# A cross-attention and expert kernel on one core: the beginning in another order, with weights loaded into the places of their low parts

## The reference

```python
q = (layernorm(x) @ Wq + bq)          # 16 heads of 32
k = (y @ Wk + bk); v = (y @ Wv + bv)  # 77 keys for each batch
attn = softmax(q k^T / sqrt(32))
x = x + relu((attn v) @ W1 + b1) @ W2 + b2          # W1 512x1024, W2 1024x512
...
xt = layernorm(x); top1 = argmax(xt @ Wg.T)
xhat = (xt - mu) * rsqrt(var + 1e-5)
y = gelu((xhat * s_e + b_e) @ w1 + bb1) @ w2 + bb2  # for the expert e = top1
x = x + y
```

## Time and profile before

| | |
|---|---|
| time, median of 3 runs | 1514.02 us (1513.26 to 1514.06) |
| the profiled execution | 1511.64 us, its span 1509.8 us, mean granted TensorE clock 0.988 |
| PE, DVE, ACT, POOL busy | 97%, 68%, 47%, 29% of the span |
| HBM read and written | 76.24 MB and 46.72 MB, 81 GB/s over the span |
| first `H` matmul of the first block | 89.38 us after the span's start |

### The profile page before, as it was taken

One profiled execution on the slowest core, in us unless ns is written; L12 is line 12 of the kernel. 1 busy time (PEld: TensorE's weight loads), 2 busy tenths in 40 slices (PEclk: granted clock), 3 DMA queues, 4 the chain that ended last, 5 costly groups with the idle time before them and its releaser, 6 DMA issues.

```text
span 1509.8 us, 23959 instructions
## 1 busy us (share of the span) xinstructions
PE 1467.3 (97%) x7764; PEld 1225.1 (81%) x7764; DVE 1034.0 (68%) x2521; ACT 713.5 (47%) x2015; POOL 431.2 (29%) x312
## 2 busy tenths in 40 slices
PE   7689999999999999999999999999999999999997
PEld 4578888888888787878788888888888878778896
DVE  5845757685867677676767686758575766558666
ACT  3534535363635364545445353635353635434554
POOL 2512131222222222212121212222222222127776
PEclk9799999999999999999999999999999999999999
DMA  9310020213020202122120301120202011558873
GB/s 237 116 56 29 1 84 1 85 28 109 15 91 29 91 29 86 42 68 60 32 88 22 99 22 57 41 89 1 84 1 84 1 57 56 188 182 285 252 232 119
DMA packets 77327, 122.70 MB, mean 81 GB/s; under 512 B 28367, under 2 KB 36832, under 8 KB 76183
## 3 DMA queue, kind: packets, MB, share of 16 engines
q1 hardware_dynamic: 66406, 87.47, 20.1%
q0 software_dynamic: 10800, 33.70, 5.8%
HBM read 76.24 MB, written 46.72 MB: 81 GB/s over the span
## 4 chain that ended last, share of the span: by engine, by line
PE 91%; DVE 4%; ACT 2%; issue 1%; DMA 1%; POOL 1%; POOLq 0%; DVEq 0%; SPq 0%; ACTq 0%
PE bank L1138 24%; PE bank L1160 23%; PE bank L956 11%; PE bank L1090 8%; PE bank L980 7%; PE bank L1053 4%; PE bank L1562 4%; PE bank L1606 4%; PE bank L1229 2%; PE bank L1545 2%; PE bank L924 2%; PE bank L1207 1%; DVE actH L1071 1%; DMA w_raw<-in_W 1%; ACT actH L1065 1%
## 5 line engine op out<-in xcount | busy, mean ns | idle before, releaser
L1160 PE MATMUL bank<-w,actH 128*128 128x512 f32 x1536 | 371.2, 393 | 0.0
L1138 PE MATMUL bank<-actA,w 128*128 128x512 f32 x1536 | 371.0, 395 | 0.0
L1138 PEld LDWEIGHTS bank<-actA,w 128*128 128x128 f32 x1536 | 285.0, 188 | 61.6
L1160 PEld LDWEIGHTS bank<-w,actH 128*128 128x128 f32 x1536 | 283.2, 188 | 54.8
L1047 POOL TENSOR_TENSOR E<-E,rc 128x1232 f32<-128x1232 f32 x64 | 145.0, 2265 | 435.0 <-DVE rc L1041 435.0
L1304 POOL DMA_INDIRECT region<-rows,pos x64 | 63.7, 995 | 457.5 <-DVE pos L1298 419.0
L956 PE MATMUL bank<-actA,wq 128*128 128x512 f32 x768 | 182.0, 390 | 0.0
L1145 ACT ACTIVATE actH<-bank,b 128x512 fp32r<-128x512 f32 x128 | 88.3, 690 | 195.8 <-PE bank L1138 195.8
L1020 ACT ACTIVATE E<-bank,mx 128x77 f32<-128x77 f32 x512 | 157.6, 365 | 40.3 <-DVE mx L989 40.3
L956 PEld LDWEIGHTS bank<-actA,wq 128*128 128x128 f32 x768 | 144.2, 188 | 30.4 <-issue 0.5
L970 DVE SCALAR_TENSOR_TENSOR actQ<-bank,bq,actQ 128x512 fp32r<-128x512 f32 x64 | 48.0, 750 | 160.0 <-ACT actQ L965 160.0
(11 more groups left out here) (168 smaller groups left out, 2055.5 us busy)
## 6 DMA issues: line engine op xcount, KB each, us to landing
rowB<-region SPq DMA_DIRECT2D x71, 258.0 KB, 3.6
xn<-in_x SPq DMA_DIRECT2D x64, 256.0 KB, 2.9
rows<-in_x SPq DMA_DIRECT2D x64, 256.0 KB, 3.2
e_raw<-in_E SPq DMA_DIRECT2D x16, 256.0 KB, 3.1
region<-padrow SPq DMA_DIRECT2D x9, 258.0 KB, 2.7
w_raw<-in_W SPq DMA_DIRECT2D x1, 2048.0 KB, 10.4
w_raw<-in_W SPq DMA_DIRECT2D x2, 1024.0 KB, 8.2
e_parts<-e_high SPq DMA_DIRECT2D x8, 256.0 KB, 2.0
```

Of the source, the lines that this page charges most:

```text
L1138: mm = pe.matmul(p[:], w, a, start=k == 0 and j == 0, stop=k == KD - 1 and j == 2)
L1160: mm = pe.matmul(p[:], a, w, start=m == 0 and j == 0, stop=m == MF - 1 and j == 2)
```

## The change

Only the beginning is altered, up to the first layer of block 0.

- The four loads of `xn` are issued first, then the setup's loads; `W1` and `W2` are loaded in it too, without a wait. `XSTAT`'s chain is emitted in one go ahead of the keys, and `XT` stands between the second and the third `KP`.
- `wq_raw`, `w1_raw` and `w2_raw` are now the low places of `wq`, `w1` and `w2`, so that a low part is the loaded weight minus its high part, in place. The low part of `wq` is made by DVE and no longer by POOL; `W1` is split in four parts of 1024 columns (ACT and POOL), two of 2048 before; `W2` in four parts of 1024, during `H` 1 to 4 of block 0, high parts by ACT and low parts by DVE. `GATE` goes to `H` 5.
- Batch 0's keys go from `k_hl` to `kbd` by four ACT copies on 32 partitions each (`KCOPY`), and no longer through DRAM; its values go from `v_hl` to `vbd` by the 24 transfers directly.
- `VP` 0 stands ahead of `Q`; `VP` 1 to 3 stand in among the scores, with `Q` 2 and 3. `XB`, `ZERO_ROWS` and `XLOAD 1` go behind the attention of block 0.

```diff
+    o[0] = w2_at
     wv_raw = staged("wv_raw", [P, KT, D])
     ctxT = staged("ctxT", [P, KT, NB * M])
...
+    wq_raw = at("wq_raw", [P, KD, D], F32, wq_at + 4 * KD * D)
+    w1_raw = at("w1_raw", [P, KD, F], F32, w1_at + 4 * KD * F)
+    w2_raw = at("w2_raw", [P, MF, D], F32, w2_at + 4 * MF * D)
...
-        step("SETUP")
+
         step("XNLOAD", 0, 0)
         step("XNLOAD", 0, 2)
+        step("SETUP")
         step("XSTAT", 0)
+        step("DRIP", SUB)
+        step("BKS")
+        step("DRAIN")
         for m in range(KD):
             step("KP", m)
-        step("DRAIN")
+            if m == 1:
+                for s in range(SUB):
+                    step("XT", 0, s)
+        step("CONV_WQ")
         step("KSTORE")
-        step("CONV_WQ")
...
+        step("KCOPY")
+        step("VP", 0)
         step("VLOAD", 0, 0)
         step("VLOAD", 0, 1)
-        step("XLOAD", 0)
-        for m in range(KD):
-            step("Q", 0, m)
-            if m in (1, 2):
-                step("CONV_W1", m - 1)
-        step("GATE")
+        step("MASKS")
+        step("Q", 0, 0)
+        step("Q", 0, 1)
+        step("CONV_W1", 0)
         for g in range(KD):
             for s in range(SUB):
                 step("S", 0, g, s)
-            if g == 2:
-                step("CONV_W2", 0)
             step("EXP", 0, g)
             if g:
                 step("SUM", 0, g - 1)
-        step("CONV_W2", 1)
-        step("ZERO_ROWS")
-        step("XLOAD", 1)
-        for s in range(SUB):
-            step("XB", 0, s)
+                step("CONV_W1", g)
+            if g + 2 < KD:
+                step("Q", 0, g + 2)
+            if g + 1 < NB:
+                step("VP", g + 1)
+                step("VSTORE", g + 1)
+        step("XLOAD", 0)
...
+            if b == 0:
+                for s in range(SUB):
+                    step("XB", 0, s)
+                step("ZERO_ROWS")
+                step("XLOAD", 1)
...
+                if b == 0 and 1 <= m <= 4:
+                    step("CONV_W2", m - 1)
+                if b == 0 and m == 5:
+                    step("GATE")
...
+        def dve_bks(dve):
             dve.wait_ge(L["first"], 16 * NFIRST)
             dve.tensor_scalar(bks[:], bk[:], SCALE, None, ALU.mult).then_inc(S["dve_bks"], 1)
...
+        def act_kcopy(act):
+
+            act.wait_ge(S["pool_zero"], 1)
+            act.wait_ge(S["act_k"], KD)
+            act.wait_ge(S["dve_k"], KD)
+            for h in range(HG):
+                q = slice(HD * h, HD * h + HD)
+                act.activation(kbd[q, :, :, M * h:M * h + M], k_hl[q, :, :, 0:M], ACT.Identity).then_inc(S["act_kbd"], 1)
...
+        def dve_conv_wq(dve):
+            dve.wait_ge(S["act_wq"], 1)
+            dve.tensor_tensor(flat(wq[:, 1]), flat(wq_raw[:]), f32(flat(wq[:, 0])), ALU.subtract
+                              ).then_inc(S["dve_wq"], 1)
...
+        def pool_conv_w1(pool, k):
+            pool.wait_ge(S["act_w1"], k + 1)
+            pool.tensor_tensor(w1[:, 1, k, :], w1_raw[:, k, :], f32(w1[:, 0, k, :]), ALU.subtract
+                               ).then_inc(S["pool_w1"], 1)
...
+                pe.wait_ge(S["act_kbd"], HG)
+                if b >= BPB:
+                    pe.wait_ge(ld_k, 16 * KLOADS * (b // BPB))
...
             if b == 0 and j == 0:
-                act.wait_ge(S["pool_wq"], 1)
-                act.wait_ge(S["pool_w1"], 2)
-                act.wait_ge(S["w2_lo"], 1)
+                act.wait_ge(st_k, 16 * 2 * (NB - 1))
+                act.wait_ge(S["act_kbd"], HG)
```

More of the change, by code:

```diff
@@ L154, in staged @@
         return at(name, shape, dt, o[0] - size(shape, dt))
+    o[0] = E_at
     wk_raw = staged("wk_raw", [P, KT, D])
+    c_raw = staged("c_raw", [P, 2 * P])
+    assert o[0] <= E_at + size([P, KD, SUB, SC], F32)
+    o[0] = w2_at
     wv_raw = staged("wv_raw", [P, KT, D])
     ctxT = staged("ctxT", [P, KT, NB * M])
[L159 to L166, removed]
+    v_f = [staged(f"v_f{i}", [M, D]) for i in range(2)]
+    bvbc = staged("bvbc", [M, D])
+    assert o[0] <= w2_at + size([P, MF, D], F32)
+    o[0] = actH_at
     k_hl = staged("k_hl", [P, 2, KD, NB * M], F32R)
     k_f = staged("k_f", [P, KD, NB * M])
[L169 to L172, removed]
+    assert o[0] <= actH_at + size([P, 2, SLOTS, BLK], F32)
+    wq_raw = at("wq_raw", [P, KD, D], F32, wq_at + 4 * KD * D)
+    w1_raw = at("w1_raw", [P, KD, F], F32, w1_at + 4 * KD * F)
+    w2_raw = at("w2_raw", [P, MF, D], F32, w2_at + 4 * MF * D)
+    assert NB == 4
+    v_hl = [at(f"v_hl{i}", [M, 2, D], F32R, (rows_at[1], xn_at)[i // 2] + i % 2 * size([M, 2, D], F32))
+            for i in range(NB)]
+    assert 2 * size([M, 2, D], F32) <= min(size([P, SUB, ROW], F32), SUB * size([P, D], F32))
     e1 = at("e1", [P, KD, NE, EH], F32, wq_at)
@@ L649, in sp_kstore @@
             for h in range(2):
-                for i in range(NB):
+                for i in range(1, NB):
                     sp.dma_start(k_parts[i, h].rearrange("g p k -> p g k"),
@@ L666, in sp_vload @@
         def sp_vload(sp, i, part):
-            if part == 0 and i == 0:
-                for n_, s_ in enumerate(st_vs):
-                    sp.wait_ge(s_, 16 * (NB // 2))
+            if i == 0:
+                sp.wait_ge(S["act_v"], 1)
+                sp.wait_ge(S["dve_v"], 1)
                 sp.wait_ge(S["pool_zero"], 2)
-            if i:
+            else:
+                sp.wait_ge(st_v, 16 * (NB - 1))
                 sp.wait_ge(S["pe_av"], 3 * NP * BPB * i)
             for c, r, k, m, h in PIECES:
-                src = v_parts[i, part, k:k + m, :].rearrange("k (g h f) -> k g h f", g=NP, h=PH)[:, :, h, :]
+                src = v_parts[i, part, k:k + m, :] if i else f32(v_hl[0][k:k + m, part, :])
                 o_ = HD * (h % HG)
-                sp.dma_start(f32(vbd[r:r + m, part, :, c, o_:o_ + HD]), src).then_inc(ld_v, 16)
+                sp.dma_start(f32(vbd[r:r + m, part, :, c, o_:o_ + HD]),
+                             src.rearrange("k (g h f) -> k g h f", g=NP, h=PH)[:, :, h, :]).then_inc(ld_v, 16)
         KLOADS, VLOADS = HG * KD, 2 * len(PIECES)
@@ L682, in sp_vstore @@
             sp.wait_ge(S["dve_v"], i + 1)
[L683 removed]
+            sp.dma_start(v_parts[i].rearrange("s k f -> k s f"), f32(v_hl[i][:])).then_inc(st_v, 16)
         def sp_e1raw(sp, e):
@@ L830, in pool_conv_wq @@
-        def pool_conv_wq(pool):
-            pool.wait_ge(S["act_wq"], 1)
-            hi, lo = (wq[:, h].rearrange("p k n -> p (k n)") for h in range(2))
-            pool.tensor_tensor(lo, wq_raw[:], f32(hi), ALU.subtract).then_inc(S["pool_wq"], 1)
-        def w1_half(h, i):
-            n = KD * F // 2
-            return w1[:, h].rearrange("p k n -> p (k n)")[:, n * i:n * i + n], w1_raw[:, n * i:n * i + n]
-        def act_conv_w1(act, i):
-            act.wait_ge(L["w1"], 16)
-            hi, raw = w1_half(0, i)
-            act.activation(hi, raw, ACT.Identity).then_inc(S["act_w1"], 1)
@@ new lines, in xattn_moe_kernel, with w2_part, act_conv_w2 @@
+        NW2 = 4
+        def w2_part(t, i):
+            n = MF // NW2
+            return flat(t[:, n * i:n * i + n, :])
+        def act_conv_w2(act, i):
+            act.wait_ge(L["w2"], 16)
+            act.wait_ge(S["dve_v"], NB)
+            act.activation(w2_part(w2[:, 0], i), w2_part(w2_raw, i), ACT.Identity).then_inc(S["act_w2"], 1)
+        def dve_conv_w2(dve, i):
+            dve.wait_ge(S["act_w2"], i + 1)
+            dve.tensor_tensor(w2_part(w2[:, 1], i), w2_part(w2_raw, i), f32(w2_part(w2[:, 0], i)), ALU.subtract
+                              ).then_inc(S["dve_w2"], 1)
@@ L1014, in act_s @@
                 return
+            if b == 0 and s == 0:
+                act.wait_ge(S["dve_tri"], 1)
             if b and s == 0:
@@ L1636, in xattn_moe_kernel @@
             "SETUP": {"sp": sp_setup, "pool": pool_setup, "dve": dve_setup},
+            "BKS": {"dve": dve_bks},
+            "MASKS": {"dve": dve_masks},
+            "KCOPY": {"act": act_kcopy},
             "XLOAD": {"sp": sp_xload},
```

102 lines of the change are left out of this document (32 added, 70 removed).

## The result

The changed kernel takes 1517.47 us (1515.24 to 1520.93, 14 runs) where the kernel before takes 1513.49 (1511.07 to 1514.89, 14 runs): 1.003 of its time, 95% interval 1.0022 to 1.0039. I had forecast 1504.6. It is slower, by 0.3%.

What follows compares the result with a forecast made beforehand. PE was taken as busy 97%, leaving idle or half-clock time before block 0's first `H`: -5.9 at `Q` and -3.5 from `Q` to `H` make -9.4, profiled 1511.64 to 1502.2, median 1504.6, range 1500.5 to 1510.

Steps and rivals of the forecast that it cites:

- The change touches only what stands ahead of that `H`, and the streams behind it stay: Block 0's first `H`, at 89.38 before: only its start time, forecast 80.0, and fitting work among `H` 1 to 5 matter.
- What is put behind: Work moved behind the first `H`: `W2`'s parts fit under `H`, row statistics slip about 1.3 with room, added wait nothing.
- my five rivals: Slow clock at first Q, dearer score phase, late loads (0.26 together), more won (0.14), slower than before (0.04).
- The one on the other side, half clock in the score phase: Scores: PE never gets full clock, `H` at 96.7, 7.3 late, 1521 us; chance 0.04.
- Up to the first Q: Block 0's start, loads to first `Q`: `Q` starts at 25.8 against 31.73, 5.9 sooner.
- the 4.48 hold: Before the first `Q`: a small DVE instruction held 4.48 beside POOL's low part of `Wq`; forecast gone.
- my first rival: PE's clock down at the first Q, taking 5.7: `H` at 83, 1507.5 us; 0.26 shared with two other rivals.
- my own signs of being wrong: PE waiting for DVE in `H`, clock 0.50 in 26 to 45, or a load ending a wait behind 20 us.
- From Q to H: Scores through `AV` to first `H`: 3.5 sooner, 9.8 + 4.5 of waits gone, new work and a 1.7 hold put in.
- The hold: `VP` 3: DVE's subtraction of `v_hl` held beside POOL's `W1` part, some 2.3 instead of 0.69, making `H` 1.7 later.
- the bounds: Spread around `H` at 80.0, between 76 and 85; full clock in last transposes and `AV` would give 3.3.
- the added wait: Ahead of each later group of scores: 60 fulfilled waits behind queued matmuls cost nothing, or 1.2 if bared.

Runs made afterwards that it cites:

- The gap alone: The kernel before with only 128 unused bytes per partition added ahead of `kbd`: 1529.89 us against 1515.63, 1.0098 of it.
- the change without the gap: The changed kernel with `wg_raw` allocated behind all other tiles, order and waits untouched: 1504.40 us, 0.9925 of the kernel before.
- `AV` aligned: The changed kernel with tiles reordered, `wg_raw` last, and the distance of `vbd` and `actH` meant as a multiple of 256 bytes too: 1502.06 us, 0.9913 of before.

## Why the prediction was wrong, point by point

**The step that failed** is "The change touches only what stands ahead of that `H`, and the streams behind it stay", and with it "What is put behind" as the whole account of the blocks behind. Their instructions stay; what one of them costs did not. 240 of the 512-column products of a block went from 226.7, 229.0 and 228.3 ns to 232.5, 232.3 and 232.4: 48 x 5.8 + 96 x 3.3 + 96 x 4.1 = 990 ns, and the block grew by 0.95 to 1.0. The gap alone gives the loss, and the change without the gap gives the gain, so it is shown that the 128 bytes between the weights and the tiles behind them are the cause. Why a distance that is not a multiple of 256 bytes slows a product is not: no record tells what PE waits for inside a matmul. The Trainium skill, "SBUF — State Buffer", "SBUF: two separate sides", says that PE never waits on anyone, and "TensorE: Matmul & The Clock Gate", "Step-by-step: what each phase is for", that loading the next weights takes nothing from the running matmul's reads. Read so, a tile's place would not matter to PE. The 1529.89 of the gap alone shows that here it does, and the measurement decides; whether PE's own two reads collide, no run here shows.

**None of my five rivals had it.** The one on the other side, half clock in the score phase, did not occur: from 31 to 55 every window shows 1.00. The clock fell again only behind the scores, and was at 0.50 for the first 4.1 of `AV`'s 6.97; before shows that too (0.50 in the windows from 71 to 75, then 0.89 and 1.00).

**Up to the first Q** (-5.9 forecast, -4.7 measured). `bks` 11.34 for 11.2; the first normalised rows at 14.7 for 14.9; the 4.48 hold gone, as forecast. Mis-sized in this trace: `Wk` at 10.50 for 8.6, and two key projections of 6.37 in all for 5.1, so that `XT` began at 16.71 for 14.9, without the wait of 1.2; the low part of `Wq` ended at 26.90 for 25.8. Part of this is the execution: with `wg_raw` last, `Wk` lands at 10.09, the two projections take 5.12 and `Q` starts at 25.33.

**The clock at the first Q** was my first rival, and came in half its size. The windows of the changed kernel (PEclk is the granted clock as a share of 2.4 GHz):

```profile
core 0: us, PE busy (x) PEld busy (x) DVE busy (x) ACT busy (x) POOL busy (x), PEclk, DMA share, GB/s
...
25.00:27.00 2.00, 0.00 (x0) 0.03 (x1) 2.00 (x2) 1.93 (x4) 0.00 (x0) 0.96 1.01 251
27.00:29.00 2.00, 2.00 (x5) 1.61 (x6) 1.30 (x4) 1.05 (x2) 0.00 (x0) 0.50 1.38 124
29.00:31.00 2.00, 2.00 (x8) 1.58 (x7) 0.16 (x2) 0.00 (x0) 0.00 (x0) 0.68 1.36 117
...
71.00:73.00 2.00, 2.00 (x6) 1.52 (x6) 1.97 (x4) 1.01 (x2) 0.00 (x0) 0.50 0.00 0
```

After 2.70 idle the clock is 0.50 until some way into 29 to 31, and the 24 `Q` take 7.30; 24 `Q` take 5.74 at full clock in this kernel, so 1.5 are lost where I had 2.9. With `wg_raw` last they took 5.72 after the same 2.70. A clock of 0.50 in 26 to 45 was one of my own signs of being wrong, and it came, in 27 to 29 and part of 29 to 31.

**From Q to H** (-3.5 forecast, -3.0 measured, with those 1.5 in it). The hold has its 2.46 for 2.3, and 0.69 once POOL's part stood behind it. So the rule that I weighed there (the Trainium skill, "SBUF — State Buffer", "Who interferes with whom") agrees with the trace. `AV` starts at 70.56 for 66.5: 1.2 of it from `Q`'s late start, 1.5 from the clock, and 1.4 that no run takes apart; hand-overs that I had not priced are my guess. From there to `H` 11.1 passed where I had put 12.8 and 0.7 of reserve. The cause is the clock, which I had only in the bounds: the last 12 transposes took 1.47 and the last 9 `AV` 2.33, at 1.00, where before has 2.79 and 3.92, at 0.50:

```profile
85.62 3.92 PE L1090 MATMUL bank<-actH,vbd 128*128 128x512 f32 x9
```

Against that, `AV`'s 21 took 6.97 for 6.38, more of them at half clock than in before, and 0.63 was idle ahead of the last 9. Two misses of opposite sign, and the sum looked better than its terms.

**Put behind H**: nothing waits in `H`, at `Y` or at the next `XT`. Right, as is the value of the added wait (nothing).

Were the blocks behind as before, the changed kernel would have stood at about 1502, by the ratio of the kernel with `wg_raw` last (0.9925 of 1513.49; 1499.6 to 1504.6 by its interval). The mechanism of the beginning was right; a cost outside of it, of some 16 us in the traces (15.4 and 0.6), was left out.

## What to carry to other kernels

When a diff touches an allocator, list which tiles moved against which, before believing that an untouched loop costs what it did; here three kinds of 512-column products were fastest when the distance of their operands was a multiple of 256 bytes, and a small tile in front of the large ones cost more than a whole reordering won. Compare a steady block of both traces by the distances of starts: a 2.5% longer matmul shows in no wait, clock or busy share. In an in-order stream, put work that nobody awaits yet (a weight's split) behind the short steps that someone does.

## What the runs showed of the hardware

- The time between 512-column float32r products depends on the distance in SBUF between their two operands: 226.7 ns (`Q`) at 0, 256 and 512 bytes beyond a multiple of 2048, 232.5 at 128 and 232.7 at 64 beyond it.
- That is so for products that wait for nobody at a granted clock of 1.00, with three kinds of product: 3.3 ns (`H`), 4.1 (`Y`) and 5.8 (`Q`) at 128 bytes. The 308-column products (`S`) stay at 141 to 142 at every distance that they had.
- The same 2.70 of idle time ahead of the first `Q` was followed by half clock in three profiled executions (7.22, 7.30 and 7.34 for 24) and by full clock in five (5.70 to 5.83). What decides was not found; this alone moves the first `H` by 1.5.
- Not settled: in the two kernels with the tile moved and `AV` aligned, one interval, from block 7 to 8, takes 82.4 to 82.5, where before has 80.3. ACT waits there 5.4, for 3.3 in before, for a load of expert weights, which SP issued 2.1 later in the block than in before, behind four loads of rows that took it 8.20 to issue where before has 6.07. Why these took longer was not followed.
